# Output projection of a 32-head attention moved out of the pair loop into seven block products whose token operands pass through DRAM

## The reference

```python
def _L0_attn_ref(hidden_states, wq, wkv, wo):
    q = jnp.einsum('bsd,de->bse', hidden_states, wq).reshape(B, S, H, DQ)
    kv = jnp.einsum('bsd,de->bse', hidden_states, wkv)
    ...
    scores = jnp.einsum('bqhd,bkhd->bhqk', q[..., :DN], k) * scale
    scores = jnp.where(causal[None, None], scores, NEG_INF)
    probs = jax.nn.softmax(scores, axis=-1)
    attn = jnp.einsum('bhqk,bkhd->bqhd', probs, v).reshape(B, S, H * DV)
    return jnp.einsum('bse,ed->bsd', attn, wo)

x = x + 0.5 * _L0_ffn_ref(_layernorm(x), ...)      # 64 experts of rank 16, the best 16 of them
x = x + _L0_attn_ref(_layernorm(x), wq, wkv, wo)
x = x + 0.5 * _L0_ffn_ref(_layernorm(x), ...)
```

## Time and profile before

| | |
|---|---|
| median of 3 runs | 1065.74 us (1065.37 to 1067.65) |
| the profiled execution | 1066.88 us |
| its span in the trace | 1064.8 us |
| busy: PE / DVE / POOL / ACT | 98% / 65% / 48% / 45% |
| granted clock of TensorE, mean | 0.996 |
| DMA | 110.11 MB, mean 103 GB/s |
| the routed layer, V products and first q and k | to 297 us |
| the pair loop up to the last pair | 297 to 922 us |
| the last pair and the rest of its output projection | 922 to 958 us |
| the routed layer again | 958 to 1064.8 us |

### The profile page before, as it was taken

One profiled execution on the slowest core, in us unless ns is written; L12 is line 12 of the kernel. 1 busy time (PEld: TensorE's weight loads), 2 busy tenths in 40 slices (PEclk: granted clock), 3 DMA queues, 4 the chain that ended last, 5 costly groups with the idle time before them and its releaser, 6 DMA issues.

```text
span 1064.8 us, 18640 instructions
## 1 busy us (share of the span) xinstructions
PE 1047.5 (98%) x5652; PEld 906.7 (85%) x5652; DVE 691.5 (65%) x1889; ACT 482.1 (45%) x1388; POOL 511.5 (48%) x444
## 2 busy tenths in 40 slices
PE   8999999999999999999999999999999999999998
PEld 7899788888778888888888888888888888879997
DVE  6778852333467777767677677676776777776552
ACT  4112455554465555555455555455554555531110
POOL 5331378995266547446465474474564643210000
PEclk9999999999999999999999999999999999999999
DMA  9700254662522213123122222131222221450000
GB/s 368 318 0 1 79 202 178 253 257 108 208 70 90 71 59 101 47 79 98 49 89 69 78 89 59 59 99 49 89 80 68 89 69 40 140 254 11 20 20 30
DMA packets 48910, 110.11 MB, mean 103 GB/s; under 512 B 5360, under 2 KB 21744, under 8 KB 47344
## 3 DMA queue, kind: packets, MB, share of 16 engines
q1 hardware_dynamic: 48880, 109.73, 29.8%
HBM read 73.79 MB, written 35.91 MB: 103 GB/s over the span
## 4 chain that ended last, share of the span: by engine, by line
PE 94%; DVE 3%; POOL 1%; ACT 1%; issue 1%; DMA 0%; POOLq 0%; DVEq 0%; ACTq 0%
PE bank L232 28%; PE bank L234 28%; PE bank L233 27%; PE bank L444 4%; PE bank L434 3%; PE bank L462 3%; PE bank L289 1%; PE bank L240 1%; POOL downT_lo L1322 1%; DVE prob L891 0%; PE bank L313 0%; DVE st L767 0%; DMA x<-x_in 0%; DVE bank L879 0%; DVE upT_lo L1567 0%
## 5 line engine op out<-in xcount | busy, mean ns | idle before, releaser
L565 ACT ACTIVATE bank<-bank,nmax 128x128 f32<-128x128 f32 (+1 forms) x256 | 101.5, 397 | 92.9 <-DVE nmax L879 92.8
L1053 POOL TENSOR_TENSOR stage_w<-stage_w 128x256 f32<-128x256 f32 x128 | 91.7, 737 | 89.4 <-DMA stage_w<-wqk 86.9
L960 DVE TENSOR_TENSOR x<-bank,x 128x512 f32<-128x512 f32 x128 | 88.0, 688 | 38.9 <-PE bank L234 38.8
L879 DVE CUSTOM_DVE_ANT_0 bank<-bank,mask 128x128 f32<-128x128 f32 (+1 forms) x256 | 83.6, 389 | 36.8 <-PE bank L234 36.8
L232 PE MATMUL bank<-wo_lo,attT_hi 128*128 128x512 f32 x256 | 100.7, 393 | 1.3 <-POOL wo_lo L1037 1.3
L234 PE MATMUL bank<-wo_hi,attT_hi 128*128 128x512 f32 x256 | 100.0, 390 | 0.0
L233 PE MATMUL bank<-wo_hi,attT_lo 128*128 128x512 f32 x256 | 99.6, 389 | 0.0
L1035 POOL CAST wq_hi<-stage_w 128x256 fp32r<-128x256 f32 (+1 forms) x31 | 28.4, 915 | 145.3 <-PE bank L234 145.3
L891 DVE TENSOR_SCALAR prob<-bank,rinv 128x128 f32<-128x128 f32 (+1 forms) x256 | 95.1, 414 | 4.5
L232 PE MATMUL bank<-xc_lo,wq_hi 128*128 128x512 f32 x224 | 94.6, 422 | 0.7 <-ACT s7q L520 0.7
L232 PE MATMUL bank<-xc_lo,wk_hi 128*128 128x512 f32 x224 | 92.3, 412 | 1.8 <-DVE s7k L919 1.5
(11 more groups left out here) (145 smaller groups left out, 2960.2 us busy)
## 6 DMA issues: line engine op xcount, KB each, us to landing
stage_w<-wqk SPq DMA_DIRECT2D x32, 512.0 KB, 3.4
keep_v<-out_hl SPq DMA_DIRECT2D x64, 256.0 KB, 2.3
v<-keep_v SPq DMA_DIRECT2D x64, 256.0 KB, 2.9
stage_v<-wv SPq DMA_DIRECT2D x4, 2048.0 KB, 8.5
stage_wo<-wo SPq DMA_DIRECT2D x16, 512.0 KB, 3.4
keep_vraw<-out_raw SPq DMA_DIRECT2D x64, 128.0 KB, 2.1
v_raw<-keep_vraw SPq DMA_DIRECT2D x64, 128.0 KB, 2.9
upT_raw<-up_w SPq DMA_DIRECT2D x4, 544.0 KB, 6.4
```

What stands on the lines that cost most here:

```text
L565: nc.scalar.activation(sp[b][:, a:e], sp[b][:, a:e], ACT.Exp, bias=nmax[:, c:c + 1], scale=-1.0, accum_out=rsum[:, c:c + 1]).then_inc(s["e ...
L879: nc.vector.tensor_tensor_reduce(out=sp[b][:, a:e], in0=sp[b][:, a:e], in1=mask[:, a:e], scale=-SCALE, scalar=BIG, op0=ALU.add, op1=ALU.mi ...
L960: nc.vector.tensor_tensor(x[:, t, :], fp[t % 2][:, :], x[:, t, :], ALU.add).then_inc(s["fill_done"], 1)
L1053: nc.gpsimd.tensor_tensor(stage_w[:, out, :], stage_w[:, a, :], stage_w[:, b, :], op).then_inc(s["w_sum_s"], 1)
```

## The change

The output projection leaves the loop. It becomes one product of Strassen's form over all 4096 features: `wo` in four blocks (2048 features by 256 outputs), the attended values in four blocks (2048 features by 512 tokens), seven block products, each summed over 16 pairs. A chunk m (0 to 55, eight for each product) is two pairs of one product; `pe_o(m, c)` is 6 matmuls, so a chunk has 12 and all have 672, where `pe_output` had 768.

In the loop ACT copies each attended unit in plain float32 (`act_attended`, no `attT_lo`), POOL makes four combinations of blocks for each pair (T3, T1, T2, N4), and SP stores seven tiles of 256 KB for each pair to DRAM (`store_att`). Scores are made two units ahead, in two pairs of banks. q and k have a staging tile each, so POOL and SP take their weights in another order.

In the new phase SP loads 512 KB of token operand for each chunk into one of four slots, ACT rounds it (`act_o_tokens`), DVE makes the rest (`dve_o_tokens`); every second chunk both do the same with 128 x 1024 elements of weights. POOL makes the weight sums S1 and S3 (8 instructions), DVE S2 and S4. Results come out transposed, so `pe_back` turns them with 32 transposes in 8 groups and `dve_back` adds them to `x`. Chunks 0 to 6 stand in the last pair. The weights of the second routed layer are read back in the midst of the phase, and its tiles go in the order 4 to 7, 0 to 3.

```diff
-        def pe_output(pe, p, t):
...
+        def pe_o(pe, m, c):
+            i, g = divmod(m, OG)
+            if c == 0:
+                if m % 2 == 0:
+                    pe.wait_ge(s["wo_split"], m // 2 + 1)
+                pe.wait_ge(s["o_split"], m + 1)
...
+            for a in range(2):
+                cols = slice(a * P, (a + 1) * P)
+                mm = mm3(banks[a][:, :], ow_hi[w][:, q, cols], ow_lo[w][:, q, cols], o_hi[n][:, c, :], o_lo[n][:, c, :],
+                         first, g == OG - 1 and c == 1, True)
+            if c == 1:
+                mm.then_inc(s["o_used"], 1)
...
+        def pe_back(pe, r):
+            if r == 0:
+                pe.wait_ge(s["av_copied"], 4 * PAIRS)
+            else:
+                pe.wait_ge(s["ct_added"], r)
...
         def pe_pair(pe, p, first=False, final=False):
...
+                pe_prob_transpose(pe, u, j)
+                if final:
+                    for n in (((0, 0), (0, 1)), ((1, 1), (2, 0)), ((3, 1), (4, 0)), ((5, 1), (6, 0)))[j]:
+                        pe_o(pe, *n)
...
+                pe.wait_ge(s["pT_split"], 2 * u + 2)
+                pe_attend(pe, p, j)
+                if j < 2:
+                    pe_scores(pe, p, j + 2)
...
+                if final:
+                    for n in (((1, 0),), ((2, 1), (3, 0)), ((4, 1), (5, 0)), ((6, 1),))[j]:
+                        pe_o(pe, *n)
...
+        def act_output(act):
+            for m in range(7, OGROUPS):
...
+                if m % 2 == 0:
+                    act_o_weight(act, m // 2)
+                act_o_tokens(act, m)
...
+        def dve_o_tokens(dve, m):
+            n = m % O_SLOTS
+            dve.wait_ge(s["o_hi_s"], m + 1)
+            lo(o_lo[n][:, :, :].rearrange("p c n -> p (c n)"), o_raw[n][:, :, :].rearrange("p c n -> p (c n)"),
+               o_hi[n][:, :, :].rearrange("p c n -> p (c n)")).then_inc(s["o_split"], 1)
...
+        def dve_output(dve):
+            for m in range(7, OGROUPS):
+                if m in (9, 11, 13, 15):
+                    dve_o_s2(dve, (m - 9) // 2)
+                elif m in (25, 27, 29, 31):
+                    dve_o_s4(dve, (m - 25) // 2)
+                elif m in (19, 43, 51):
+                    dve_o_sum(dve, {19: 0, 43: 1, 51: 2}[m])
+                elif m in (22, 24, 46, 48):
+                    dve_back(dve, {22: 0, 24: 1, 46: 2, 48: 3}[m])
...
+        def pool_wo_sums(pool):
...
+            pool.wait_ge(s["scores_ready"], 8 * PAIRS)
+            for h in range(4):
+                nc.gpsimd.tensor_tensor(wo_rows(S1, h), wo_rows(A21, h), wo_rows(A22, h), ALU.add).then_inc(s["wo_s1_s"], 1)
+                pool.wait_ge(s["wo_s1_s"], h + 1)
+                nc.gpsimd.tensor_tensor(wo_rows(S3, h), wo_rows(A11, h), wo_rows(A21, h), ALU.subtract).then_inc(s["wo_s3_s"], 1)
...
+        def load_tokens(sp_, m):
+            i, g = divmod(m, OG)
+            op, n = O_TOKEN[i], m % O_SLOTS
+            if m >= O_SLOTS:
+                sp_.wait_ge(s["o_used"], m - O_SLOTS + 1)
...
@@ block sync
+            load_wo_first(sync, 1)
+            load_tokens(sync, 1)
+            load_wo(sync, 0, "wo_a11")
+            load_tokens(sync, 2)
+            load_tokens(sync, 3)
+            load_pair(sync, LAST, final=True)
+            load_wo(sync, 1, "wo_a21")
+            load_wo(sync, 3, "wo_a22")
+            for m in range(4, 7):
+                load_tokens(sync, m)
+            load_wo(sync, 2, "wo_a12")
+            for m in range(7, OGROUPS):
+                load_tokens(sync, m)
+                if m == 4 * OG:
...
+                        sync.dma_start(t[:, :, :].rearrange("p k n -> p (k n)").bitcast(F32), keep_down[i]).then_inc(s["downagain_loaded"], 16)
+                elif m == 5 * OG:
+                    sync.wait_ge(s["wo_split"], 20)
+                    for i, t in enumerate((upT_hi, upT_lo)):
+                        sync.dma_start(t[:, :, :].rearrange("p k n -> p (k n)").bitcast(F32), keep_up[i]).then_inc(s["upagain_loaded"], 16)
@@ block tensor
+            for m in range(7, OGROUPS):
+                if m in (18, 20, 42, 44, 49, 51):
+                    pe_back(pe, {18: 0, 20: 1, 42: 2, 44: 3, 49: 4, 51: 5}[m])
+                elif m == 54:
+                    pe_ffn_transpose(pe, NT)
+                pe_o(pe, m, 0)
+                pe_o(pe, m, 1)
```

More of the change, by code:

```diff
@@ new lines, in build_macaron @@
+        wo_s1 = place("wo_s1", [P, PAIRS, 2 * P], F32, at=where["upT_hi"])
+        WO = {A11: wo_raw[:, 0, :, :], A21: wo_raw[:, 1, :, :], A12: wo_raw[:, 2, :, :], A22: wo_raw[:, 3, :, :],
+              S1: wo_s1[:, :, :], S2: wo_raw[:, 0, :, :], S4: wo_raw[:, 2, :, :]}
+        slot = 2 * 2 * P * 16
+        at = where["wq_hi"]
+        o_hi, o_lo, o_raw, ow_hi, ow_lo, ow_raw = [], [], [], [], [], []
+        for i, a in enumerate((early, at, at + slot, at + 3 * slot)):
+            o_hi.append(place(f"o_hi{i}", [P, 2, HALF], F32R, at=a))
+            o_lo.append(place(f"o_lo{i}", [P, 2, HALF], F32R, at=a + slot // 2))
+            o_raw.append(place(f"o_raw{i}", [P, 2, HALF], F32, at=a + slot // 2))
@@ new lines, in build_macaron @@
+        for i, a in enumerate((at + 4 * slot, at + 5 * slot, at + 2 * slot)):
+            ow_hi.append(place(f"ow_hi{i}", [P, 4, 2 * P], F32R, at=a))
+            ow_lo.append(place(f"ow_lo{i}", [P, 4, 2 * P], F32R, at=a + slot // 2))
+            ow_raw.append(place(f"ow_raw{i}", [P, 4, 2 * P], F32, at=a + slot // 2))
+        csum = [place("csum0", [P, HALF], F32, at=at + 6 * slot), place("csum1", [P, HALF], F32, at=where["xa"])]
+        os17 = place("os17", [P, 2, HALF], F32, at=where["v"])
@@ L415, in pe_v, with o_uses @@
             mm.then_inc(s[v_ready(i)], 1)
-        def pe_output(pe, p, t):
[L419 to L425, removed]
+        def o_uses(m):
+            return 32 if m % OG == OG - 1 else 16
@@ new lines, in pe_back @@
+        def pe_back(pe, r):
[3 more added lines that the diff above has]
+                pe.wait_ge(s["ct_added"], r)
+            if r % 2 == 0:
+                if r < 6:
+                    pe.wait_ge(s["o_sum"], r + 2)
+                else:
+                    pe.wait_ge(s["o_c12"], 2)
+            for k in range(2):
+                t = 2 * (r % 2) + k
+                for a in range(2):
+                    last = nc.tensor.transpose(ct[:, (2 * k + a) * P:(2 * k + a + 1) * P],
+                                               csum[a][:, t * P:(t + 1) * P], ident[:])
+            last.then_inc(s["ct_ready"], 1)
@@ new lines, in dve_o_s4, with dve_o_sum @@
+        def dve_o_s4(dve, h):
+            dve.wait_ge(s["wo_s2_s"], h + 1)
+            nc.vector.tensor_tensor(wo_rows(S4, h), wo_rows(A12, h), wo_rows(S2, h), ALU.subtract).then_inc(s["wo_s4_s"], 1)
+        def dve_o_sum(dve, block):
+            i = (1, 4, 5)[block]
+            dve.wait_ge(s["o_used"], OG * (i + 1))
+            dve.wait_ge(s[("o_snap1", "o_snap7", "o_snap2")[block]], 2)
+            if block > 0:
+                dve.wait_ge(s["ct_ready"], 2 * block)
+            for a in range(2):
+                nc.vector.tensor_tensor(csum[a][:, :], (oacc if i in O_ACC else oyz)[a][:, :],
+                                        (os2 if block == 2 else os17)[:, a, :], ALU.add).then_inc(s["o_sum"], 1)
```

633 lines of the change are left out of this document (393 added, 240 removed).

## The result

The changed kernel takes 1103.6 us (median of 4 executions, 1099.8 to 1105.8), the kernel before, on the same chip, 1066.7. The ratio is 1.034, its interval 1.031 to 1.038. The output projection moved into its own phase, with an eighth of its matmuls saved, makes the kernel 37 us slower. 1098.5 was predicted, in a range of 1075 to 1111; as a difference, +32.7 us was said and +36.9 measured.

The account below looks back on a forecast made before the run. PE's own program, busy 98% of the span, was taken as the bound. Terms -21.8 + 3.5 - 4.4 + 12.8 + 19.5 + 4.1 + 13.0 + 6 gave +32.7 us on 1066.9: 1099.6 profiled, 1098.5 median, range 1075 to 1111.

Parts of the forecast that it names:

- Products, turning back, old waits: 672 matmuls in place of 768, -21.8 us; transposing results back, +3.5; last pair's old waits gone, -4.4.
- The loop: Iteration without output tiles falls from 42.2 to 31.3 us, PE covering the other engines; bounds 0 and 1 us an iteration.
- First operands: Last pair: chunk 0 is ready 4.3 us after the transposes, which take 0.7; PE waits 3.6 us.
- Chunk 4: Last pair: tokens 4 queue behind 8.75 MB, so the chunk starts at 28.4 us and not 20.6; 7.8 us.
- Chunks 7 to 15: After the last pair: POOL's sums and DVE's instructions take turns at the port; 44.1 us for 24.6 of PE work, +19.5.
- Turning back: New phase: pe_back at chunks 20, 44 and 49 waits for DVE's additions or sums; +4.1 us.
- Reloads: Chunks 33 and 41: tokens queue behind 4 MB of down and 4.25 MB of up weights, 6.2 and 6.8 us; +13.0.
- Clock: PE runs near 1.2 GHz after long new pauses in the last pair and new phase; +6 us, bounds 0 and 10.
- B: Chunks 7 to 15: DVE goes on between POOL's instructions and S3 comes in time; -17 us and 1.5 of clock, 1080; chance 0.10.
- C: Last pair and new phase: reloads and wo blocks cost token loads nothing; -13.0, -7.8, -3 of clock, 1075; chance 0.08.
- D: Loop: PE no longer covers DVE and ACT, each iteration waits 0.5 to 1 us; 1106 to 1113; chance 0.12.
- A: New phase: four slots suffice, neither port nor queue costs as said, new waits stay under 22.7 us; 1051; chance 0.10.

Follow-up runs that it names:

- The last version: Changed kernel with sums on DVE, wo blocks in quarters, reloads in pieces, and four turning transposes one chunk later: 1059.3 us, ratio 0.9944 to the kernel before.
- the run in quarters: Changed kernel with wo blocks A21, A22 and A12 loaded in 0.5 MB quarters, two behind each of token loads 4 to 9: 1093.6 us.
- unread sums: Changed kernel with weights S3 and S1 taken raw, S2 made from A22, while POOL still writes eight sums that nobody reads: 1105.0 us.

## Why the prediction was right

It was right in sign, size and mechanism, 5 us low, or 4 as a difference to the kernel before. Behind the loop 55.4 us of losses were said and 59 came. The sum is closer than some of its terms, whose errors cancel in part; that much is luck. By its own terms:

- **Products, turning back, old waits** (-22.7): not measured by a run. The trace has the rates: 48 matmuls of chunks 12 to 15 in 10.96 us, 0.228 us each where 0.227 was said, and 0.44 us for a turn. The last version, with 9.7 us of waits, is 7.7 us below the kernel before.
- **The loop**: 31.3 us said, 31.47 measured, the units 8.5, 8.8, 7.1 and 7.1 us apart. "I cost all this at nothing", with 0 to 1 us as bounds, was nearly right. In unit 1 the first matmul behind the transposes takes 0.50 us of the chain and not 0.23, probably because ACT is copying `s7q` out of its bank at that time; this was not tested. Over 15 pairs the loop is 2.6 us longer than said, and the first iteration waits 1.2 us for `qT_lo`, which I had not seen. POOL's four new instructions take 1.30 us each there, as said.
- **First operands**: 3.6 said, 3.7 measured.
- **Chunk 4**: 7.8 said, 8.2 measured, and the run in quarters shows the cause. Both ends of this wait lie 2 us later than said (PE comes 22.6 us into the pair and not 20.6, the operands at 30.7 and not 28.4), so the good number is a difference of two errors. The last pair takes 44.9 us where 41.3 was said. The window of 800 to 810 us has a clock of 0.63, so part of the difference is what I had counted under clock.
- **Chunks 7 to 15**: 44.1 us said. Chunk 7 could start at 815.6 and chunk 16 starts at 859.3 (the turn ahead of chunk 18 at 864.76 less two chunks of 2.73): 43.7. The number is right, the path to its end is not. A turn costs 3.3 us and not 2.41 + 1.22 = 3.6, so DVE is clear of POOL sooner, and the last chunk that waits for it is 11, at 843.96 us. From there PE itself sets the time and not, as said, the last sum and chunk 15: five chunks of 2.73 us and 1.7 us of half clock.
- **Turning back**: 4.1 said; 3.0 waited (1.3 for `x` at chunks 20 and 44, 1.7 for `csum` at chunk 49).
- **Reloads**: 13.0 said, 8.3 + 7.2 = 15.5 measured, 2.5 more. This is the largest error in a wait, and the step is "14.6, are ready at 17.1". Tokens 33 landed at 913.4 us, 16.7 after the end of chunk 28: SP issued the reload 1.2 us behind tokens 32, not at once, and the 4 MB took 12.1 us from tokens 32 at 900.0 to 912.1, not 10.0.
- **Clock**: +6 said. In the trace of the changed kernel the clock is 0.50 behind the waits of 7 to 8 us ahead of chunks 4, 33 and 41, and still 1.00 behind the 3.7 us ahead of chunk 0. But kept at full clock behind both reloads, the kernel gained 1.2 us at most of the 4 us that the rule of the term gives there: the term was too high for the reloads. For the last pair it was probably too low, as its 3.6 us too much and a clock of 0.63 suggest; no run separates that.

Of the rivals, B (no turns at the port) fell with DVE at 3.4 us beside unread sums, C (the queue lets tokens through) with 11 to 20 us for a 512 KB load, D (the loop a chain) with 31.47 us. A was 1051; the kernel with the cures comes to 1059, so the lead of four slots nearly holds once queue and port are free.

## What to carry to other kernels

Work moved out of a loop takes its operands with it: cost the queue that brings them, not only the eighth of the matmuls saved. A large transfer goes into a queue of small ones in pieces that cost no more than their spare time; here another queue did not replace that. Where DVE and POOL would both work with two SBUF inputs side by side, try the work on DVE, even if it is the busier one, as long as its own duration fits: here a sum costs DVE 1.22 us of its own, or 2.2 when POOL makes it.

## What was not expected of the hardware

- DVE and POOL, both with full queues, alternate strictly, one instruction each: eight pairs in 26.5 us, 3.3 us a pair, which is less than the sum of their durations alone, 2.41 and 1.22.
- Two queues share DMA engines by packets: in 6 us each got 150, 15 KB packets of one against 2 KB of the other, and a 512 KB load took 12 us, as if it stood behind the large one.
- A clock of 0.50 over 4 us behind a wait made PE 2.0 us later at the next late load, but only 1.1 us later behind it.
